# Another order of the steps in two attention stages of an eight-stage kernel on one Trainium2 core

## Chip, cores and metric

One core of one Trainium2 chip runs the whole program. The metric is the device time of the program in microseconds (us), the median of several executions; lower is better.

## What is computed

The reference is a stack of eight residual sublayers on x of shape (16, 128, 128), all in float32: four attentions, each followed by a feed-forward layer.

```python
x = x + tanh(g_xattn[0]) * attention0(layernorm(x), ctx, ctx)   # 16 heads of 8, window of 64
x = x + tanh(g_ffn[0])   * experts0(layernorm(x))               # 8 experts, top 2
x = x + tanh(g_xattn[1]) * attention1(ctx, layernorm(x))        # 8 heads of 64, rotary keys
x = x + tanh(g_ffn[1])   * experts1(layernorm(x))               # 16 experts, top 2, and a shared one
x = x + tanh(g_xattn[2]) * attention2(layernorm(x), ctx)        # 16 heads of 8, q, k, v projected
x = x + tanh(g_ffn[2])   * gated_layer(layernorm(x))
x = x + tanh(g_xattn[3]) * correlation(layernorm(x), ctx, ctx)
x = x + tanh(g_ffn[3])   * experts3(layernorm(x))               # 8 experts, top 2
```

The change concerns attention0 and attention2, "the first" and "the third" attention below. Both compute softmax(q kT / sqrt(8)) v for 16 heads of 8 over 128 queries and 128 keys for each of the 16 batches, and then a 128 x 128 output projection. The first masks scores further than 64 from the diagonal and takes q, k and v as they are. The third projects them first.

## The kernel before

Each stage is a block in which five engines run their own instruction lists, kept in step by semaphores alone. A stage treats one batch (128 tokens x 128 features) at a time and is written as a software pipeline by hand: `walk(engine, [(step, lag), ...])` issues for t = 0, 1, 2, ... each listed step in the listed order for batch t - lag. So the table of an engine sets which instruction stands behind which on that engine, and by how many batches the steps lie apart. One pass through a table is called a round; in the steady state every engine makes one round for each batch. An engine works in order: a step that waits holds everything behind it. The lags have a meaning only within one engine, since nothing but the semaphores ties the engines together.

Both attentions are `small_head_attention` (`project=False` for the first, `project=True` for the third). Its steps, with the lines of the profile:

- TensorE (PE): `in_T` transposes the normalised x (L585); `qkv` projects it in the third (L609, L610, L611, in this order q, k, v); `scores(0)` and `scores(2)` make the scores of heads 0 to 7 and 8 to 15 in PSUM banks 0, 1 and 2, 3 (L530, and the mask's product L527 ahead of it in the first); `probs(0)` and `probs(2)` transpose the exponentials (L556); `pv` multiplies with the values (L593); `output_transpose` (L543), `out_T` (L563) and `out` (L599) lead to the projected output; in the first, `next_T` (L571) transposes the normalised result, `logits` (L603) makes the router's logits of it and `ranks` (L284 to L287) counts tokens per expert.
- VectorE (DVE): `stats_in` (L240, L242; in the third with the addition of the last expert layer's two late results ahead of it, L352), `norm_in` (L252), `maximum(0)` and `maximum(1)` over the two halves of the scores (L629), `shift(0)` and `shift(1)`, which subtract the maximum and so free the PSUM banks (L638), `divide` (L646, L649), `add` of the residual (L654), `values` in the third (L685); in the first `stats_out`, `norm_out` (L252 into `routed_lines`), `chosen` (L261 to L267, the top two experts) and `placed` (L273, L277, their line numbers).
- ScalarE (ACT): the exponentials (L746), and copies out of PSUM, among them `queries` (in the third keys L774, then queries L780), `outputs` (L787), `out_T` (L758), `next_T` (L763), `logits` (L791) and `probs_out` (L753).
- GpSimd (POOL): `dev_in` and `dev_out` (the inverse deviations, L246, L248; in the third also a copy of the context, L701), `bias` (L705), `spread_keys` (L715: the keys times the head mask into a 128 x 512 tile), `spread_values` (L722), and DMAs by index: `sent` (L313, the routed lines of a batch, two of them) in the first and `fetched` (L345, the late results, two of them) in the third; `counted` (L300) in the first.

The scores have no second buffer. `scores(0)` of a batch waits for `shift(0)` of the batch before, and `scores(2)` for its `shift(1)`:

```python
wait(pe, s.keys, b + 1)
wait(pe, s.shifted, b * 2 + (first // 2 - 1))
```

`spread_keys` of batch b waits for both parts of the scores of batch b - 2, and in the third for the keys of batch b (`s.kT`). `fetched` of batch b waits until the late results of batch b - 2 are added. `chosen` waits for the logits that ACT has copied, `placed` and `counted` for the ranks, `sent` for the slots that `placed` writes.

Of the kernel before, what the change touches and what calls it, by code (L numbers as in the profile page):

```python
# [72 lines left out]
def split(ap, b):  # L73
    return ap.rearrange("p (a b) -> p a b", b=b)
# [375 lines left out]
def small_head_attention(nc, sems, k, tag, src, masked, project, w_out, tg, tgb, w_gate, n_gate, ld, a):  # L450
# [40 lines left out]
    with nc.Block() as block:  # L491
# [27 lines left out]
        def _(pe):  # L519
# [27 lines left out]
            def probs(first):  # L547
                def stage(b, sl):
                    wait(pe, s.exp, b + 1)
                    for g in range(first, first + 2):  # L550
                        wait(pe, s.pT, b * NG + (g - 1))
                        if g == 0:
                            wait(pe, s.ots, b)
                        for j in range(HG):
                            h = g * HG + j
                            last = nc.tensor.transpose(bank[:, PT + g % 2, j * T:(j + 1) * T],  # L556
                                                       k.e[:, sl, h * T:(h + 1) * T], c["ident"])
                        last.then_inc(s.ptr, 1)
                return stage
# [46 lines left out]
            def qkv(b, sl):  # L606
# [4 lines left out]
                nc.tensor.matmul(bank[:, MA, 384:512], ctxs[:, sl, :], k.w["wv2"], start=True, stop=True).then_inc(s.qkv, 1)  # L611

            pe.wait_ge(ld.weights[4 if project else 0], 16)
            walk(pe, [(out_T, 5), (scores(0), 2), (qkv, 1), (out, 5), (pv, 4), (scores(2), 2),
                  (probs(0), 3), (output_transpose, 4), (probs(2), 3), (in_T, 0)]
                 if project else
                 [(ranks, 7), (scores(0), 1), (logits, 6), (probs(0), 3), (output_transpose, 4), (in_T, 0), (probs(2), 3),
                  (out_T, 4), (scores(2), 1), (out, 4), (pv, 3), (next_T, 5)])

        @block.vector  # L620
        def _(dve):
            nc.vector.memset(vpad, 0.0).then_inc(s.padded, 1)
            dve.wait_ge(s.padded, 1)
            nc.vector.memset(vpad[:, :, :, DH:DH + 1], 1.0).then_inc(s.padded, 1)  # L624

            def maximum(half):
                def stage(b, sl):
                    wait(dve, s.scores, b * 2 + (half + 1))
                    nc.vector.tensor_reduce(mx[:, sl, 8 * half:8 * half + 8],  # L629
                                            bank[:, 2 * half:2 * half + 2, :].rearrange("p g (j t) -> p (g j) t", j=HG),  # L630
                                            AX.X, ALU.max).then_inc(s.max, 1)
                return stage

            def shift(half):
                def stage(b, sl):
                    wait(dve, s.max, b * 2 + (half + 1))
                    wait(dve, s.ptr, b * NG - NG)
                    nc.vector.tensor_tensor(split(k.e[:, sl, 1024 * half:1024 * half + 1024], T),  # L638
                                            bank[:, 2 * half:2 * half + 2, :].rearrange("p g (j t) -> p (g j) t", j=HG),
                                            over(mx[:, sl, 8 * half:8 * half + 8], T, 2), ALU.subtract).then_inc(s.shifted, 1)  # L640
                return stage

            def divide(b, sl):
# [12 lines left out]

            def stats_in(b, sl):
                if project:
                    add_late(dve, b)
                elif b % 4 == 0:  # L660
                    dve.wait_ge(ld.x[b // 4], 16)
                stats1(dve, at(k.x, b), sl, b + 1, s.xh)

            def norm_in(b, sl):
                wait(dve, s.xTp, b - 1)
                norm1(dve, xh[:, sl, :], at(k.x, b), sl, b + 1).then_inc(s.xh, 1)

            def stats_out(b, sl):
                wait(dve, s.added, b + 1)
                stats2(dve, at(k.x, b), sl, b + 1, s.xh2)  # L670

            def norm_out(b, sl):
                line_free(dve, s, ld, 0, b)
                norm2(dve, k.line[:, b % LINES, :, 0:D], over(k.x[:, b, :], 2, 1), sl, b + 1).then_inc(s.xh2, 1)

            def chosen(b, sl):
                choose(dve, b)

            def placed(b, sl):
                place(dve, b, bank[:, MA, 256:256 + n_gate])  # L680

            def values(b, sl):
                wait(dve, s.qkv, b + 1)
                wait(dve, s.q, b + 1)
                nc.vector.tensor_tensor(at(vtok, b), bank[:, MA, 384:512], k.rows["b_v"], ALU.add).then_inc(s.v, 1)  # L685

            walk(dve, [(shift(1), 4), (norm_in, 1), (stats_in, 0), (maximum(0), 3), (add, 6), (shift(0), 3),
                  (values, 2), (maximum(1), 3), (divide, 5)]
                 if project else
                 [(shift(0), 3), (add, 6), (stats_out, 6), (placed, 8), (maximum(1), 3), (stats_in, 0), (shift(1), 3),  # L690
                  (divide, 5), (norm_out, 6), (chosen, 7), (maximum(0), 2), (norm_in, 0)])

        @block.gpsimd
        def _(pool):
            pool.wait_ge(s.padded, 2)

            def dev_in(b, sl):
                dev1(pool, sl, b + 1)
                if project:
                    wait_apart(pool, k, s.qkv, b - 1)  # L700
                    nc.gpsimd.tensor_copy(ctxs[:, sl, :], at(k.ctxT, b)).then_inc(s.ctxs, 1)  # L701

            def bias(b, sl):
                wait_apart(pool, k, s.xh, b + 1)
                nc.gpsimd.tensor_tensor(at(k.x, b), at(k.x, b), tgb, ALU.add).then_inc(s.biased, 1)  # L705

            def dev_out(b, sl):
                dev2(pool, sl, b + 1)

            def spread_keys(b, sl):  # L710
                if project:
                    wait(pool, s.kT, b + 1)
                wait_apart(pool, k, s.scores, b * 2 - 2)
                keys = kT[:, sl, :] if project else at(k.ctxT, b)
                nc.gpsimd.tensor_tensor(kx[:, sl, :, :], over(keys, HG, 1), over(c["headmask"], T, 2),  # L715
                                        ALU.mult).then_inc(s.keys, 1)

            def spread_values(b, sl):
                if project:
                    wait(pool, s.v, b + 1)  # L720
                wait_apart(pool, k, s.pv, b - 1)
                nc.gpsimd.tensor_copy(vpad[:, sl, :, 0:DH], split(at(vtok, b), DH)).then_inc(s.vpad, 1)  # L722

            def counted(b, sl):
                count(pool, b)

            def sent(b, sl):
                if b == 0:
                    pool.wait_ge(ld.empty[0], 32 * (E0 + 1))
                send(pool, b)  # L730

            def fetched(b, sl):
                fetch(pool, b)

            if not project:
                begin(pool)
            walk(pool, [(fetched, -1), (dev_in, 0), (spread_values, 3), (spread_keys, 1), (bias, 4)]
                 if project else
                 [(dev_in, 0), (spread_keys, 0), (dev_out, 5), (bias, 0), (counted, 7), (spread_values, 3),
                  (sent, 8)])  # L740

        @block.scalar
        def _(act):
# [45 lines left out]
            def logits(b, sl):  # L789
# [1 line left out]
                nc.scalar.activation(at(k.logits, b)[:, 0:n_gate], bank[:, MB, 384:384 + n_gate],  # L791
                                     ACT.Copy).then_inc(s.logits_out, 1)

            walk(act, [(queries, 1), (outputs, 4), (probs_out, 3), (in_T, 0), (out_T, 4), (exps, 2)]
                 if project else
                 [(outputs, 4), (logits, 6), (probs_out, 3), (queries, 0), (out_T, 4), (exps, 2), (next_T, 5)])

# [1233 lines left out]
```

## Time and profile before

| | us |
|---|---|
| median of three executions (lowest, highest) | 1074.42 (1074.01, 1080.66) |
| the profiled execution | 1072.74 |
| its span in the profile | 1071.0 |
| PE busy | 818.7 (76%) |
| DVE busy | 648.2 (61%) |
| ACT busy | 500.8 (47%) |
| POOL busy | 437.2 (41%) |
| first attention, first DVE statistics to the last indexed send | 15.6 to 176.8 |
| third attention, first DVE memset to the last addition | 630.6 to 773.2 |

The time of the profiled execution is the whole program's; the span is from its first to its last instruction. Busy shares are averages over eight stages with different limits, so a stage is read by itself, through the rows of its own stretch. A stretch of the profile is named by its microseconds from the start of the span. PEld is TensorE's weight load, which runs ahead of the matmuls and whose starts follow one another more evenly, so distances on PE are read there.

### The profile page before, as it was taken

To read this page: it belongs to the slowest core of one execution; us is meant where nothing else is said; L and a number is where in the kernel's file an instruction comes from. 1 tells how busy PE (TensorE), PEld (TensorE's weight loads), DVE (VectorE), ACT (ScalarE), POOL (GpSimd) and SP (SyncE) were. 2 spreads that over 40 slices of the span, in tenths; PEclk is the share of its full clock that TensorE was granted. 3 is DMA by queue.
4 is the path that set the end of the run, shared out by engine and by line. 5 is a ranking of instruction groups with operands and counts; after the bars stand their busy time and mean duration, and the time that the engine had idled before them with its cause. 6 is when DMAs were issued, how large, how long until landed. Compare 5 with 4: busy or idle time off the path is not lost. (4 is left out here: it accounts for less than half of the span.)

```text
span 1071.0 us, 20849 instructions
## 1 busy us (share of the span) xinstructions
PE 818.7 (76%) x5970; PEld 588.4 (55%) x5984; DVE 648.2 (61%) x1891; ACT 500.8 (47%) x1403; POOL 437.2 (41%) x779
## 2 busy tenths in 40 slices
PE   4998882995789989898727949999787546259991
PEld 1556561663457777677515735666566335237771
DVE  5898973333357777777534438999598344334443
ACT  1565560552156656665504724777534122025552
POOL 3355644002334455653340036665265128803334
PEclk9999995998699999999958976999968765579996
DMA  8999601331000000000002530010001211122214
GB/s 276 369 403 340 230 22 34 83 79 38 11 11 11 7 17 22 16 17 12 16 26 58 117 78 21 17 22 12 1 2 40 79 41 36 44 57 59 58 36 130
DMA packets 68861, 78.93 MB, mean 74 GB/s; under 512 B 12432, under 2 KB 58144, under 8 KB 68496
## 3 DMA queue, kind: packets, MB, share of 16 engines
q1 hardware_dynamic: 59840, 62.74, 18.3%
q0 software_dynamic: 6368, 13.38, 4.4%
q10 hardware_dynamic: 2544, 1.48, 0.6%
q8 instruction: 53, 0.87, 0.4%
q14 instruction: 56, 0.46, 0.1%
HBM read 31.61 MB, written 45.96 MB: 72 GB/s over the span
## 5 line engine op out<-in xcount | busy, mean ns | idle before, releaser
L313 POOL DMA_INDIRECT routed_region<-routed_lines,line_slots x96 | 97.2, 1012 | 23.2 <-issue 22.6
L345 POOL DMA_INDIRECT late_results<-routed_region,line_slots x64 | 63.2, 987 | 97.8 <-DVE work_a L624 80.4
L248 POOL TENSOR_TENSOR small<-small,half_and_eps 128x1 f32<-128x1 f32 x160 | 92.3, 577 | 12.5
L753 ACT ACTIVATE probs_keymajor_a<-banks 128x512 f32<-128x512 f32 x128 | 70.0, 595 | 43.0 <-PE banks L556 43.0
L868 PE MATMUL banks<-work_a,weights_a 128*128 128x128 f32 x512 | 76.8, 295 | 15.5 <-ACT work_a L1084 9.7
L1244 PE MATMUL banks<-weights_f,block_feat_f 128*128 x156 | 83.7, 619 | 1.2 <-ACT block_feat_f L1296 0.9
L530 PE MATMUL banks<-work_a 32*128 32x512 f32 x256 | 81.1, 713 | 0.0
L629 DVE TENSOR_REDUCE small<-banks 128x8 f32<-128x1024 f32 x64 | 77.5, 1212 | 5.7 <-PE banks L530 5.6
L868 PEld LDWEIGHTS banks<-work_a,weights_a 128*128 128x128 f32 x512 | 65.3, 200 | 25.8 <-ACT work_a L1084 13.4
L638 DVE TENSOR_TENSOR exps_a<-banks,small 128x1024 f32<-128x1024 f32 x64 | 77.6, 1213 | 2.3 <-PE banks L556 1.9
L556 PE MATMUL banks<-consts,exps_a 128*128 128x128 f32 x512 | 72.5, 288 | 1.3 <-ACT work_a L787 1.3
L1261 PE MATMUL banks<-weights_f,block_hidden_feat_f 128*128 x468 | 65.8, 277 | 7.3 <-ACT block_hidden_feat_f L1316 7.1
L246 POOL TENSOR_TENSOR small<-small,half_and_eps 128x1 f32<-128x1 f32 x160 | 31.6, 198 | 94.8 <-DVE small L242 94.0
L556 PEld LDWEIGHTS banks<-consts,exps_a 128*128 128x128 f32 x512 | 59.4, 149 | 19.6 <-issue 15.9
L1426 DVE TENSOR_TENSOR block_hidden_f<-block_gate_f,banks 128x64 f32<-128x64 f32 (+1 forms) x86 | 26.8, 312 | 71.4 <-ACT block_gate_f L1302 70.4
L1479 POOL DMA_INDIRECT expert_results<-block_out_f,block_to_f x39 | 37.8, 970 | 76.5 <-DVE block_to_f L1436 42.9
L1316 ACT ACTIVATE block_hidden_feat_f<-banks,cols 128x128 f32<-128x128 f32 x156 | 44.7, 374 | 40.2 <-PE banks L1252 29.1
L1261 PEld LDWEIGHTS banks<-weights_f,block_hidden_feat_f 128*128 128x128 f32 x468 | 58.4, 192 | 9.0 <-issue 9.0
L746 ACT ACTIVATE exps_a<-exps_a 128x2048 f32<-128x2048 f32 x32 | 61.5, 1921 | 3.2 <-DVE exps_a L638 3.2
L1252 PEld LDWEIGHTS banks<-consts,block_hidden_f 128*128 128x128 f32 x281 | 37.5, 143 | 44.0 <-issue 28.2
L1077 ACT ACTIVATE probs_keymajor_a<-banks 128x512 f32<-128x512 f32 x64 | 34.9, 595 | 51.5 <-PE banks L894 51.5
L1096 ACT ACTIVATE exps_a<-banks,small 128x256 f32<-128x256 f32 x128 | 58.7, 492 | 0.0
(277 smaller groups left out, 2002.8 us busy)
## 6 DMA issues: line engine op xcount, KB each, us to landing
routed_region<-mid_a SPq DMA_DIRECT2D x52, 528.0 KB, 13.8
block_lines_f<-routed_region SPq DMA_DIRECT2D x125, 66.0 KB, 1.9
routed_region<-block_out_f SPq DMA_DIRECT2D x86, 64.0 KB, 1.8
weights_f<-in_weights_f SPq DMA_DIRECT2D x1, 4096.0 KB, 15.7
weights_f<-in_weights_f SPq DMA_DIRECT2D x3, 1024.0 KB, 12.4
shifted_rows<-work_a SPq DMA_DIRECT2D x16, 128.0 KB, 1.7
both_outs_f<-expert_results SPq DMA_DIRECT2D x4, 512.0 KB, 5.7
routed_region<-routed_lines,line_slots POOLq DMA_INDIRECT x96, 2.3
```

The lines of the kernel that those rows point to most:

```text
L248: nc.gpsimd.tensor_tensor(rstd[:, s, 1:2], rstd[:, s, 0:1], k.half[:, 0:1], ALU.pow).then_inc(sem.rstd, 1)
L313: nc.gpsimd.indirect_dma_start(k.regions[layer % 2], bass.IndirectOffsetOnAxis(k.slots[:, b, j:j + 1], 0), k.line[:, b % LINES, j, :], Non ...
L345: nc.gpsimd.indirect_dma_start(k.late[:, b % 2, j, :], None, k.regions[layer], bass.IndirectOffsetOnAxis(k.slots[:, b, j:j + 1], 0)).then_ ...
L530: last = nc.tensor.matmul(bank[:, g, :], qT[rows_, sl, :], kx[rows_, sl, :, :].rearrange("p j t -> p (j t)"), start=not masked, stop=True)
L556: last = nc.tensor.transpose(bank[:, PT + g % 2, j * T:(j + 1) * T], k.e[:, sl, h * T:(h + 1) * T], c["ident"])
L629: nc.vector.tensor_reduce(mx[:, sl, 8 * half:8 * half + 8], bank[:, 2 * half:2 * half + 2, :].rearrange("p g (j t) -> p (g j) t", j=HG), A ...
L638: nc.vector.tensor_tensor(split(k.e[:, sl, 1024 * half:1024 * half + 1024], T), bank[:, 2 * half:2 * half + 2, :].rearrange("p g (j t) -> ...
L746: nc.scalar.activation(k.e[:, sl, :], k.e[:, sl, :], ACT.Exp, scale=float(1 / np.sqrt(DH))).then_inc(s.exp, 1)
L753: nc.scalar.activation(k.pT[:, g * 512:(g + 1) * 512], bank[:, PT + g % 2, :], ACT.Copy).then_inc(s.pT, 1)
L868: last = nc.tensor.matmul(bank[:, MA, p * T:(p + 1) * T], k.w[weight][:, p * 128:(p + 1) * 128], kvT[:, sl, part * T:(part + 1) * T], star ...
L1244: nc.tensor.matmul(bank[:, 2 + m % 2, 0:wide], k.gotT[:, m % 2, :], ups[:, bass.ds(offs[m], wide)], start=True, stop=True).then_inc(s.up, 1)
L1261: last = nc.tensor.matmul(bank[:, 6 + m % 2, 0:D], k.hidT[:, m % 2, i * T:(i + 1) * T], downs[:, bass.ds(offs[m] + (down_at + i * D), D)], ...
```

## The change

Only the tables of `walk` are changed, for all four engines in both attentions; no step is edited, added or removed. In the third, the two parts of the scores now stand next to one another on PE, as do the two maxima and the two shifts on DVE; the fetch of the late results on POOL moves from one batch ahead of `dev_in` to two. In the first, `ranks` comes a round earlier on PE, `norm_in` on DVE a round later than `stats_in`, and `divide` behind `maximum(0)`.

```diff
-            walk(dve, [(shift(1), 4), (norm_in, 1), (stats_in, 0), (maximum(0), 3), (add, 6), (shift(0), 3),
-                  (values, 2), (maximum(1), 3), (divide, 5)]
+            walk(dve, [(shift(0), 3), (shift(1), 3), (divide, 5), (values, 2), (norm_in, 1), (maximum(0), 2),
+                       (maximum(1), 2), (add, 5), (stats_in, 0)]
...
-            walk(pool, [(fetched, -1), (dev_in, 0), (spread_values, 3), (spread_keys, 1), (bias, 4)]
+            walk(pool, [(dev_in, 2), (bias, 3), (spread_values, 4), (fetched, 0), (spread_keys, 2)]
...
```

Third attention, PE, one steady round; before:

```order
L563 MATMUL banks<-consts,work_a 128x128
L530 MATMUL banks<-work_a 128x512 x2
L609 MATMUL banks<-work_a,weights 128x128
L610 MATMUL banks<-work_a,weights 128x128
L611 MATMUL banks<-weights,work_a 128x128
L599 MATMUL banks<-weights,work_a 128x128
L593 MATMUL banks<-probs_keymajor_a,work_a 32x128 x16
L530 MATMUL banks<-work_a 128x512 x2
L556 MATMUL banks<-consts,exps_a 128x128 x8
L543 MATMUL banks<-consts,work_a 128x128 x4
L556 MATMUL banks<-consts,exps_a 128x128 x8
L585 MATMUL banks<-consts,work_a 128x128
```

The same round after the change:

```order
L530 MATMUL banks<-work_a 128x512 x4
L585 MATMUL banks<-consts,work_a 128x128
L563 MATMUL banks<-consts,work_a 128x128
L593 MATMUL banks<-probs_keymajor_a,work_a 32x128 x16
L609 MATMUL banks<-work_a,weights 128x128
L610 MATMUL banks<-work_a,weights 128x128
L611 MATMUL banks<-weights,work_a 128x128
L599 MATMUL banks<-weights,work_a 128x128
L556 MATMUL banks<-consts,exps_a 128x128 x8
L543 MATMUL banks<-consts,work_a 128x128 x4
L556 MATMUL banks<-consts,exps_a 128x128 x8
```

The projection of the next batch (L609 to L611) and the output projection (L599) stood between the two parts of the scores and now stand behind both, and behind `pv`.

Third attention, DVE, one steady round; before:

```order
L638 TENSOR_TENSOR exps_a<-banks,small 128x1024
L252 TENSOR_SCALAR work_a<-x_tok,small 128x128
L352 SCALAR_TENSOR_TENSOR x_tok<-late_results,expert_shares,x_tok 128x128 x2
L240 BN_STATS small<-x_tok 128x6
L242 BN_AGGR small<-small 128x2
L629 TENSOR_REDUCE small<-banks 128x8
L654 SCALAR_TENSOR_TENSOR x_tok<-banks,tanh_gates,x_tok 128x128
L638 TENSOR_TENSOR exps_a<-banks,small 128x1024
L685 TENSOR_TENSOR work_a<-banks,rows 128x128
L629 TENSOR_REDUCE small<-banks 128x8
L646 RECIPROCAL small<-banks 128x16
L649 TENSOR_TENSOR work_a<-banks,small 128x128
```

The same round after the change:

```order
L638 TENSOR_TENSOR exps_a<-banks,small 128x1024 x2
L646 RECIPROCAL small<-banks 128x16
L649 TENSOR_TENSOR work_a<-banks,small 128x128
L685 TENSOR_TENSOR work_a<-banks,rows 128x128
L252 TENSOR_SCALAR work_a<-x_tok,small 128x128
L629 TENSOR_REDUCE small<-banks 128x8 x2
L654 SCALAR_TENSOR_TENSOR x_tok<-banks,tanh_gates,x_tok 128x128
L352 SCALAR_TENSOR_TENSOR x_tok<-late_results,expert_shares,x_tok 128x128 x2
L240 BN_STATS small<-x_tok 128x6
L242 BN_AGGR small<-small 128x2
```

The addition of the residual (L654), which waits for `out`, stood between a maximum and a shift of the two different halves; now it stands right ahead of the late results (L352), and these ahead of the two shifts.

First attention, DVE, from `shift(1)` on; before:

```order
L638 TENSOR_TENSOR exps_a<-banks,small 128x1024
L646 RECIPROCAL small<-banks 128x16
L649 TENSOR_TENSOR work_a<-banks,small 128x128
L252 TENSOR_SCALAR routed_lines<-x_tok,small 128x2x128
L261 MAX top_values<-logits 128x8
L263 MAX_INDEX top_indices<-top_values,logits 128x8
L267 TENSOR_TENSOR one_hot<-top_indices,expert_numbers 128x2x8
L629 TENSOR_REDUCE small<-banks 128x8
L252 TENSOR_SCALAR work_a<-x_tok,small 128x128
L638 TENSOR_TENSOR exps_a<-banks,small 128x1024
L654 SCALAR_TENSOR_TENSOR x_tok<-banks,tanh_gates,x_tok 128x128
```

The same stretch after the change:

```order
L638 TENSOR_TENSOR exps_a<-banks,small 128x1024
L261 MAX top_values<-logits 128x8
L263 MAX_INDEX top_indices<-top_values,logits 128x8
L267 TENSOR_TENSOR one_hot<-top_indices,expert_numbers 128x2x8
L629 TENSOR_REDUCE small<-banks 128x8
L646 RECIPROCAL small<-banks 128x16
L649 TENSOR_TENSOR work_a<-banks,small 128x128
L252 TENSOR_SCALAR work_a<-x_tok,small 128x128
L638 TENSOR_TENSOR exps_a<-banks,small 128x1024
L273 TENSOR_TENSOR picked_slots<-one_hot,banks 128x2x8
L277 TENSOR_REDUCE line_slots<-picked_slots 128x2
L252 TENSOR_SCALAR routed_lines<-x_tok,small 128x2x128
```

The choice of experts (L261 to L267) stood behind the division; now the division (L646, L649) stands behind the choice and a maximum. On PE, in the same rounds, the logits (L603) follow `next_T` (L571) with one part of the scores and `in_T` between; after the change that stretch reads:

```order
L571 MATMUL banks<-consts,routed_lines 128x128
L527 MATMUL banks<-mask_bias 128x512 x2
L530 MATMUL banks<-work_a 128x512 x2
L585 MATMUL banks<-consts,work_a 128x128
L603 MATMUL banks<-weights_a,work_a 128x8
L556 MATMUL banks<-consts,exps_a 128x128 x8
L543 MATMUL banks<-consts,work_a 128x128 x4
L556 MATMUL banks<-consts,exps_a 128x128 x8
L284 MATMUL banks<-picks_so_far,ones_and_earlier 128x8
```

Before, L585 stood ahead of the second L556 and L284 right behind L571.

## Rows read from the trace of the kernel before

**Rows 1.** Busy time by stretch: steady rounds of the first and third attention.
```profile
46.60:139.50 92.90, 85.74 (x835) 55.22 (x844) 85.58 (x199) 58.26 (x109) 52.45 (x100) 0.98 0.85 311
664.00:757.80 93.80, 90.57 (x925) 61.38 (x917) 86.45 (x155) 71.40 (x128) 53.62 (x93) 1.00 0.07 16
```
**Rows 2.** Residual additions L654, first twelve of the first, first thirteen of the third.
```profile
L654 DVE SCALAR_TENSOR_TENSOR x_tok<-banks,tanh_gates,x_tok x12: 334/339/343, 46.6 to 139.5; 128x128 f32<-128x128 f32 x12
L654 DVE SCALAR_TENSOR_TENSOR x_tok<-banks,tanh_gates,x_tok x13: 341/342/343, 671.9 to 757.6; 128x128 f32<-128x128 f32 x13
```
**Rows 3.** Timeline of PEld in the third attention: start, duration, engine, line.
```profile
691.07 0.30 PEld L609 LDWEIGHTS banks<-work_a,weights 128*128 128x128 f32 x2 [0.76 <-issue]
...
691.73 0.30 PEld L599 LDWEIGHTS banks<-weights,work_a 128*128 128x128 f32 x2
692.15 0.81 PEld L593 LDWEIGHTS banks<-probs_keymajor_a,work_a 128*32 128x32 f32 x32
693.16 0.30 PEld L530 LDWEIGHTS banks<-work_a 32*128 32x128 f32 x4 [0.20 <-issue]
```
**Rows 4.** Timeline of PEld and ACT in the first attention.
```profile
74.82 0.14 PEld L563 LDWEIGHTS banks<-consts,work_a 128*128 128x128 f32 x1
...
75.56 0.30 PEld L530 LDWEIGHTS banks<-work_a 32*128 32x128 f32 x4 [0.42 <-issue]
76.61 0.30 PEld L599 LDWEIGHTS banks<-weights_a,work_a 128*128 128x128 f32 x2 [0.76 <-ACT work_a L758]
...
80.42 0.30 PEld L603 LDWEIGHTS banks<-weights_a,work_a 128*128 128x128 f32 x2 [0.76 <-issue]
...
80.84 0.18 ACT L791 ACTIVATE logits<-banks 128x8 f32<-128x8 f32 x1 [1.26 <-PE banks L603]
```
**Rows 5.** Timeline of DVE in the first attention, the same round.
```profile
74.14 0.26 DVE L646 RECIPROCAL small<-banks 128x16 f32<-128x16 f32 x1 [0.17 <-PE banks L543]
74.43 0.29 DVE L649 TENSOR_TENSOR work_a<-banks,small 128x128 f32<-128x128 f32 x1
...
74.96 0.16 DVE L261 MAX8 top_values<-logits 128x8 f32<-128x8 f32 x1
...
75.52 1.22 DVE L629 TENSOR_REDUCE small<-banks 128x8 f32<-128x1024 f32 x1
76.65 0.34 DVE L252 TENSOR_SCALAR work_a<-x_tok,small 128x128 f32<-128x128 f32 x1
```
**Rows 6.** Timeline: `out` on PE with nothing ahead of it, then the addition.
```profile
152.55 0.49 PE L599 MATMUL banks<-weights_a,work_a 128*128 128x128 f32 x2 [0.48 <-ACT work_a L758]
...
153.08 0.35 DVE L654 SCALAR_TENSOR_TENSOR x_tok<-banks,tanh_gates,x_tok 128x128 f32<-128x128 f32 x1 [0.51 <-PE banks L599]
```
**Rows 7.** Timeline of DVE in the third attention, late results and statistics.
```profile
691.36 0.74 DVE L352 SCALAR_TENSOR_TENSOR x_tok<-late_results,expert_shares,x_tok 128x128 f32<-128x128 f32 x2 [0.27 <-DMA late_results<-routed_region,line_slots]
692.18 0.29 DVE L240 BATCH_NORM_STATS2 small<-x_tok 128x6 f32<-128x128 f32 x1
...
692.61 1.19 DVE L629 TENSOR_REDUCE small<-banks 128x8 f32<-128x1024 f32 x1
```
**Rows 8.** Timeline of ACT and POOL in the third attention: keys, then their spreading.
```profile
692.68 0.35 ACT L774 ACTIVATE work_a<-banks,cols 128x128 f32<-128x128 f32 x1
...
693.11 1.04 POOL L715 TENSOR_TENSOR work_a<-work_a,consts 128x512 f32<-128x512 f32 x1 [2.10 <-ACT work_a L774]
```
**Rows 9.** Timeline, start of the third attention: POOL L715 and DVE L352 at once.
```profile
642.01 1.05 POOL L715 TENSOR_TENSOR work_a<-work_a,consts 128x512 f32<-128x512 f32 x1
642.52 1.07 DVE L352 SCALAR_TENSOR_TENSOR x_tok<-late_results,expert_shares,x_tok 128x128 f32<-128x128 f32 x2 [0.36 <-DMA late_results<-routed_region,line_slots]
```
**Rows 10.** Timeline, first attention: POOL L715 and DVE L252 at once.
```profile
84.84 1.04 POOL L715 TENSOR_TENSOR work_a<-ctx_feat,consts 128x512 f32<-128x512 f32 x1 [0.80 <-PE banks L530]
84.87 1.09 DVE L252 TENSOR_SCALAR work_a<-x_tok,small 128x128 f32<-128x128 f32 x1
```
**Rows 11.** The indexed sends L313 from 165 to 177 us.
```profile
L313 POOL DMA_INDIRECT routed_region<-routed_lines,line_slots x8: 962/962/1092, 166.6 to 175.9; - x8
```

More of the change, by code:

```diff
@@ L613, in _ @@
             pe.wait_ge(ld.weights[4 if project else 0], 16)
-            walk(pe, [(out_T, 5), (scores(0), 2), (qkv, 1), (out, 5), (pv, 4), (scores(2), 2),
-                  (probs(0), 3), (output_transpose, 4), (probs(2), 3), (in_T, 0)]
+            walk(pe, [(scores(0), 1), (scores(2), 1), (in_T, 0), (out_T, 4), (pv, 3), (qkv, 0), (out, 4),
+                      (probs(0), 2), (output_transpose, 3), (probs(2), 2)]
                  if project else
-                 [(ranks, 7), (scores(0), 1), (logits, 6), (probs(0), 3), (output_transpose, 4), (in_T, 0), (probs(2), 3),
-                  (out_T, 4), (scores(2), 1), (out, 4), (pv, 3), (next_T, 5)])
+                 [(scores(0), 1), (in_T, 0), (logits, 6), (probs(0), 3), (output_transpose, 4), (probs(2), 3),
+                  (ranks, 6), (out_T, 4), (scores(2), 1), (out, 4), (pv, 3), (next_T, 5)])
         @block.vector
@@ L685, in values @@
                 nc.vector.tensor_tensor(at(vtok, b), bank[:, MA, 384:512], k.rows["b_v"], ALU.add).then_inc(s.v, 1)
-            walk(dve, [(shift(1), 4), (norm_in, 1), (stats_in, 0), (maximum(0), 3), (add, 6), (shift(0), 3),
-                  (values, 2), (maximum(1), 3), (divide, 5)]
+            walk(dve, [(shift(0), 3), (shift(1), 3), (divide, 5), (values, 2), (norm_in, 1), (maximum(0), 2),
+                       (maximum(1), 2), (add, 5), (stats_in, 0)]
                  if project else
-                 [(shift(0), 3), (add, 6), (stats_out, 6), (placed, 8), (maximum(1), 3), (stats_in, 0), (shift(1), 3),
-                  (divide, 5), (norm_out, 6), (chosen, 7), (maximum(0), 2), (norm_in, 0)])
+                 [(norm_out, 8), (stats_in, 0), (add, 7), (maximum(1), 4), (stats_out, 7), (shift(1), 4),
+                  (chosen, 8), (maximum(0), 3), (divide, 6), (norm_in, 1), (shift(0), 3), (placed, 8)])
         @block.gpsimd
@@ L736, in _ @@
                 begin(pool)
-            walk(pool, [(fetched, -1), (dev_in, 0), (spread_values, 3), (spread_keys, 1), (bias, 4)]
+            walk(pool, [(dev_in, 2), (bias, 3), (spread_values, 4), (fetched, 0), (spread_keys, 2)]
                  if project else
-                 [(dev_in, 0), (spread_keys, 0), (dev_out, 5), (bias, 0), (counted, 7), (spread_values, 3),
-                  (sent, 8)])
+                 [(dev_out, 7), (counted, 8), (spread_values, 5), (bias, 4), (spread_keys, 1), (sent, 8),
+                  (dev_in, 0)])
         @block.scalar
@@ L792, in logits @@
                                      ACT.Copy).then_inc(s.logits_out, 1)
-            walk(act, [(queries, 1), (outputs, 4), (probs_out, 3), (in_T, 0), (out_T, 4), (exps, 2)]
+            walk(act, [(in_T, 0), (out_T, 4), (outputs, 3), (queries, 0), (probs_out, 2), (exps, 1)]
                  if project else
-                 [(outputs, 4), (logits, 6), (probs_out, 3), (queries, 0), (out_T, 4), (exps, 2), (next_T, 5)])
+                 [(out_T, 5), (exps, 3), (next_T, 6), (outputs, 4), (queries, 0), (logits, 6), (probs_out, 3)])
 def latent_attention(nc, sems, k, ld):
```

## The prediction, made before the changed kernel ran

> **What bounds the kernel now.** I read the stretches first, then one steady round of each stage in the timeline, engine by engine. In the steady rounds of both stages PE and DVE are each busy over 92% of the time [rows 1]: 85.74 and 85.58 of 92.90 us in the first attention, 90.57 and 86.45 of 93.80 us in the third. A busy PE says little, so what counts is the loop of waits that repeats each round. The residual additions mark the rounds [rows 2]. In the first, twelve of them stand in 92.9 us, 8.45 us a round. In the third, thirteen stand in 85.7 us, 7.14 us a round.
>
> In the first, DVE hardly waits. Its largest loss is a collision: `norm_in` takes 0.34 us [rows 5], but 1.09 us when it starts just behind POOL's `spread_keys` [rows 10], and the DVE instruction behind it starts when POOL's ends. One such pair stands there, and there are four between the first and the twelfth addition, so 4 x 0.75 = 3.0 us. The granted clock of 0.98 in that stretch [rows 1] means about 3.7 us at the lower level, worth at most 1.9 us; I take 1.5 and keep it in both kernels. That leaves (92.9 - 3.0 - 1.5) / 11 = 8.04 us for a plain round.
>
> No instruction is added, so all costs below come from what stands behind what. They are worked out against the profiled execution, 1072.7 us with a span of 1071.0, which lies 1.7 us under the median; the difference is then put on the median, 1074.4.
>
> **Third attention, rounds.** The new order closes one long loop. DVE's `shift(1)` must end before PE's `scores(2)`; behind these PE has `in_T`, `out_T`, `pv`, `qkv` and only then `out`; DVE's `add` waits for `out`, and behind `add` stand the late results, the statistics and both shifts. Step by step: the first shift 1.13 and the second 1.22 and a hand-over of 0.04 [rows 5, 6] (a pass over 1024 columns lasts 1.22, its successor starts 1.13 after it); one part of the scores 1.05 [rows 4]; two transposes 0.14 each [rows 4]; `pv` 1.01, `qkv` 0.66 [rows 3]; `out` to `add` 0.53 [rows 6]; `add` 0.3 (0.34 less some overlap); late results 0.82 and statistics 0.43 [rows 7]. The sum is 7.5 us, against 7.14 now. Before, `out` was issued right behind `qkv` and ahead of `pv`, and DVE had two passes of other work on either side of `add`, so DVE's own work and not this loop set the round. The wait for the late results' DMA, 0.27 us in the row of rows 7, goes, since they are fetched a round earlier; that gain is swallowed by the loop.
>
> **Third attention, a collision in each round.** Count from the load of `qkv`. Its third product is loaded at 0.44 and ends at 0.44 + 0.49 + 0.04 = 0.97 (products as in rows 6); ACT's keys follow, and POOL's `spread_keys` starts 0.43 after them [rows 8], at 1.40, since POOL waits for the keys already now, 2.10 us in that row. It runs to 2.44. On DVE `add` starts at 0.66 + 0.53 = 1.19 and the first late addition at about 1.46. So each round `spread_keys` and the late additions want to run together. Where they did so at the start of the stage [rows 9], the pair of additions took 1.07 us instead of 0.74 [rows 7], with POOL 0.51 us ahead; with POOL only 0.06 ahead I expect the first addition to wait for nearly all of the 1.04 us, as `norm_in` did in rows 10. Should the addition start first, the second of the pair meets the same wait. The bounds are 0 and 1.0 us a round; I take 0.8, nearest to rows 10. The round is then 8.3 us.
>
> The Trainium skill, SBUF — State Buffer, section "Who interferes with whom", states that a DVE instruction with two SBUF inputs contends with a GpSimd instruction that reads SBUF, and that whichever issues first blocks the other for its whole length. L352 has two such inputs. Rows 9 agree in kind (0.33 us more). By the rule the wait is what is left of POOL's 1.04 us, about 1.0; without it the round would stay at 7.5.
>
> **Third attention, sum.** Eleven rounds of 8.3 and a last one without late results, statistics, projection and collision, 8.3 - 0.82 - 0.43 - 0.66 - 0.8 = 5.6, make 96.9 us between first and thirteenth addition, against 85.7: +11.2. Ahead of the first addition the pipeline fills at the lower clock, with both parts of the scores in a row ahead of all else: I take +1, bounds -1 and +4. At the end, the second shift of the last batch stands right behind the first instead of behind a maximum (1.13), the values and a division, some 1.9 us in all by the like rows of rows 5: -2. Sum +10.
>
> **First attention, rounds.** DVE's own list gets shorter waits, but here too a new loop closes, since `divide` now stands behind `chosen`, and `chosen` needs the logits of the same round: `out` 0.42 and `pv` 1.01 [rows 3], `next_T` with the mask to the scores' load 0.74, scores 1.05, `in_T` 0.14, logits to ACT 0.42, ACT 0.18 and 0.04 [rows 4], `chosen` 0.56, `maximum(0)` 1.13, reciprocal 0.29, quotient 0.29 and 0.04 [rows 5], `out_T` to the next scores 0.74, scores 1.05 [rows 4]. The sum is 8.10 us, 0.06 more than a plain round now: +0.7 over eleven. In this loop PE waits at `out_T` and DVE at `chosen`. The collision with `norm_in` goes: `spread_keys` is released by the scores' end, 0.29 + 0.33 + 0.74 + 1.2 = 2.6 us behind the reciprocal (1.2 is an estimate: the 1.05 of the scores and a hand-over), while `norm_in` starts 0.5 us behind it and `norm_out` 2.2 us behind it, both ahead of POOL: -3.0.
>
> **First attention, end.** POOL ends with eight sends, 166.6 to 175.9, 1.33 apart [rows 11], four batches that it could not send earlier because `sent` stood a round behind `counted`. Now both have one lag, and two batches are left: -5.3 at best. But `norm_out` of the last batch stands behind `placed` of the one before, and the last batch's own transpose, logits, choice, ranks and slots come in sequence ahead of its two sends. I take -2, bounds 0 and -5.3. Sum of the first: -4.3.
>
> Together +5.7 us: 1078.4 on the profiled execution, 1080.1 on the median.
>
> **Rivals.** (A) The late additions aren't held. For it: one row alone shows them held, and by 0.33 us, and a shift of 0.4 us of `spread_keys` would miss them. Against it: rows 10, where the wait is nearly whole. Then eleven times 0.8 goes: 1071.3. (B) In the first, `norm_out` meets `spread_keys`: it is only 0.4 us ahead, and `counted`, `spread_values` or `bias` on POOL may hold `norm_in` long enough. It decides once DVE loses 0.4 us between division and `norm_out`. Then DVE's list of 7.5 and a wait of 0.9 make 8.4: +3.3, 1083.4. (C) The other side, clearly slower: PE waits about 1.4 us in each round of the third (8.3 less 0.966 x 7.14 = 6.9 of work, rows 1 and 2), and its granted clock, 1.00 now [rows 1], falls to the lower of its two levels, 1.2 GHz. PE's part of the loop is 3.5 us, so a round at that clock costs up to 3.5 more; 2 us for six of the rounds is +12, 1092. Against it: the waits are short and PE is busy four fifths of the time. It decides if the clock falls for more than two rounds. (D) Both loops are shorter than I read them (a step released earlier): the first near 7.7 and the third near 7.0 without a collision, 1061. The waits in the code speak against it.
>
> **Numbers.** Forecast 0.46, A 0.27, B 0.12, C 0.09, D 0.06. The forecast's own bounds: the collision 0.5 to 1.0 (-3, +2), the fill (-2, +3), the first's end (-3, +2): 1075 to 1085. The range takes in A and most of B: 1068 to 1088. This kernel's measurement can tell about 1% from no change, 10.7 us. Faster by more: D and little else, 0.06. Slower by more, above 1085: C and part of B and of the forecast's upper end, 0.17. Within 1%: 0.77.
>
> **What would show it.** In the third: additions about 8.3 us apart; `add` preceded by a wait for L599; L352 pairs of some 1.5 us; L715 starting within 0.2 us of them; no wait for the late DMA; PE idle ahead of L530. In the first: L261 waiting for L791 each round, rounds of 8.1 us, no L252 over 0.6 us, and fewer sends behind the last addition. L352 pairs of 0.74 us would make A right; rounds under 7.4 in the third or under 7.9 in the first would show a loop wrong; a granted clock under 0.95 in the third would be C.

## The result and the profile after

The changed kernel takes 1087.96 us (median of 8, 1083.34 to 1095.48), the kernel before 1074.61 us in the same series (8 runs, 1072.96 to 1080.66). The ratio is 1.0124, 95% interval 1.0097 to 1.0150: the change makes the kernel slower by 13.4 us. The profiled execution took 1095.48 us, the slowest of the eight and 7.5 above their median, with a span of 1093.7.

The stretches that answer to [rows 1], of after; columns as there, the granted clock third from the end:

```profile
46.60:134.00 87.40, 84.74 (x817) 53.22 (x830) 80.33 (x199) 58.96 (x109) 55.39 (x104) 1.00 0.92 331
664.00:781.00 117.00, 101.69 (x885) 69.13 (x883) 95.12 (x160) 71.26 (x125) 53.31 (x95) 0.87 0.06 13
```

The first attention's clock is full and its twelve additions stand in 87.2 us instead of 92.9, 7.92 a round (8.00 in most). In the third the clock fell from 1.00 to 0.87, and thirteen additions stand in 110.9 us instead of 85.7.

One round of the third on DVE, the answer to [rows 7], then the POOL instruction beside it:

```profile
708.36 0.35 DVE L654 SCALAR_TENSOR_TENSOR x_tok<-banks,tanh_gates,x_tok 128x128 f32<-128x128 f32 x1 [0.52 <-PE banks L599]
708.62 1.53 DVE L352 SCALAR_TENSOR_TENSOR x_tok<-late_results,expert_shares,x_tok 128x128 f32<-128x128 f32 x2
710.19 0.29 DVE L240 BATCH_NORM_STATS2 small<-x_tok 128x6 f32<-128x128 f32 x1
...
710.62 2.33 DVE L638 TENSOR_TENSOR exps_a<-banks,small 128x1024 f32<-128x1024 f32 x2
```

```profile
708.59 1.03 POOL L715 TENSOR_TENSOR work_a<-work_a,consts 128x512 f32<-128x512 f32 x1 [2.32 <-ACT work_a L774]
```

The pair L352 takes 1.53 us instead of 0.74, with L715 0.03 us ahead of it. `add` waits for L599, and no wait for the late DMA is left. That is the predicted round. The same round and the next one on PE:

```profile
706.15 1.08 PE L593 MATMUL banks<-probs_keymajor_a,work_a 128*32 128x128 f32 x32
...
711.97 2.98 PE L530 MATMUL banks<-work_a 32*128 32x512 f32 x8 [1.37 <-DVE exps_a L638]
...
715.50 1.94 PE L593 MATMUL banks<-probs_keymajor_a,work_a 128*32 128x128 f32 x32
717.37 0.80 PE L609 MATMUL banks<-work_a,weights 128*128 128x128 f32 x2
```

PE waits 1.37 us for the shifts; in the scores behind that wait everything begins to take nearly twice as long (`pv` 1.94 instead of 1.08). The clock comes back later and falls again, but not behind every such wait. Of nine waits of 1.35 us or more in the stretch 664 to 781, seven are followed by a fall within 3 us. Two are not: the one of 1.49 us that ends at 703.6 and the one of 1.35 us that ends at 741.2, as the first and the last of these rows show (the middle one is the round that starts at 711.97):

```profile
703.60:711.90 8.30, 6.99 (x70) 4.71 (x70) 7.64 (x14) 5.64 (x10) 4.27 (x8) 1.00 0.08 17
712.00:723.00 11.00, 10.25 (x72) 6.83 (x73) 7.60 (x14) 5.80 (x10) 4.78 (x9) 0.69 0.06 14
741.20:749.50 8.30, 7.00 (x70) 4.73 (x70) 7.59 (x14) 5.64 (x10) 4.61 (x9) 1.00 0.08 17
```

So the additions follow one another in 8.2 to 8.5 us (four rounds, full clock) or in 9.9 to 11.2 (seven rounds). The waits of the stretch 664 to 781 (in total, times, longest):

```profile
DVE x_tok L654 <- PE banks L599: 19.9, 12, 3.3
...
PE banks L530 <- DVE exps_a L638: 15.1, 12, 1.5
```

In sum, against the profiled execution of before: the first attention's last addition came 3.9 us and its last send 6.6 us earlier; at the third's first transpose (L585) 0.8 us of that were left, the rest was given back in the layers between; the third's first addition came 1.9 us earlier, then +25.2 us to the thirteenth, -1.4 to the last, +0.7 behind: +22.7, as the spans say. The medians show 13.4 of it.

### The profile page after: what moved, and what is told of

It reads as the page before. It is cut to its first block and busy times, and to the rows that moved or that the text cites. A ratio compares the mean times of both kernels' runs of the same rounds, so it can differ in the third digit from the quotient of the medians.

```text
span 1093.7 us, 20849 instructions
## 1 busy us (share of the span) xinstructions
PE 836.7 (77%) x5970; PEld 602.3 (55%) x5984; DVE 650.8 (60%) x1891; ACT 503.7 (46%) x1403; POOL 436.4 (40%) x779
## 5 line engine op out<-in xcount | busy, mean ns | idle before, releaser
L313 POOL DMA_INDIRECT routed_region<-routed_lines,line_slots x96 | 96.8, 1008 | 25.8 <-issue 21.7
L345 POOL DMA_INDIRECT late_results<-routed_region,line_slots x64 | 63.2, 987 | 100.7 <-DVE work_a L624 83.2
L530 PE MATMUL banks<-work_a 32*128 32x512 f32 x256 | 78.0, 723 | 19.1 <-DVE exps_a L638 17.4
L556 PE MATMUL banks<-consts,exps_a 128*128 128x128 f32 x512 | 72.9, 289 | 0.9 <-ACT work_a L787 0.8
L556 PEld LDWEIGHTS banks<-consts,exps_a 128*128 128x128 f32 x512 | 61.5, 151 | 5.7 <-issue 1.9
L1041 POOL TENSOR_TENSOR work_a<-work_a 128x512 f32<-128x512 f32 x16 | 20.2, 1265 | 96.7 <-issue 80.3
```

The costliest lines, as they stand in the source:

```text
L313: nc.gpsimd.indirect_dma_start(k.regions[layer % 2], bass.IndirectOffsetOnAxis(k.slots[:, b, j:j + 1], 0), k.line[:, b % LINES, j, :], Non ...
L345: nc.gpsimd.indirect_dma_start(k.late[:, b % 2, j, :], None, k.regions[layer], bass.IndirectOffsetOnAxis(k.slots[:, b, j:j + 1], 0)).then_ ...
L530: last = nc.tensor.matmul(bank[:, g, :], qT[rows_, sl, :], kx[rows_, sl, :, :].rearrange("p j t -> p (j t)"), start=not masked, stop=True)
```

## The experiments

Each ratio is to the kernel before on the same chip, with its 95% interval. Four series ran on four chips: E1 to E4, E5 to E8, E9 to E11, E12. The trace also has the time at which each semaphore is raised; "released" below is that time.

**E1, E2: one attention each.** The tables of before were put back in the third (E1) or in the first (E2).

> The first attention's tables are the new ones, the third's are those of before. Theory 1 (the gain of the first attention is real and stays): its last addition and last send come 4 and 6.6 us earlier, as in the trace of after, and the whole is 6 us faster than before, 1068 to 1069. Theory 2 (what is won there is given back in the expert layer and the second attention, as 3.1 of 6.6 us were in after's trace by the start of the second expert layer, and 5.9 by its end): 1073 to 1075.

> The third attention's tables are the new ones, the first's are those of before. Theory 1 (the two parts add up): after minus before is +13.4 us in the medians, and with the first's -6.6 out it is +19 to +20, 1094. Theory 2 (my forecast's sizes, +10 for the third): 1084 to 1085. In the trace: rounds of 8.2 us with a full TensorE clock and of 9.9 with half of it in part, for theory 1; 8.3 throughout for theory 2.

E1: 1.0004 (0.9981 to 1.0026). E2: 1.0172 (1.0150 to 1.0194). So the loss is the third's: 18.6 us, near the 19 to 20 of theory 1. The first's gain was missing, and not for the reason expected: its last addition came at 167.2 us, not at 160.6, with 2.9 us lost among the first twelve additions and 3.1 in the last four. Two things stand out in it. In two rounds `norm_out` (L252) took 1.27 and 1.25 us beside `spread_keys`, rounds of 9.5 and 9.6: rival B, in part. And in the last rounds ACT's `next_T` started long after PE's transpose:

```profile
146.46 0.33 PE L571 MATMUL banks<-consts,routed_lines 128*128 128x128 f32 x1
148.54 0.39 PE L603 MATMUL banks<-weights_a,work_a 128*128 128x8 f32 x2 [1.75 <-ACT work_a L763]
```

```profile
148.21 0.28 ACT L763 ACTIVATE work_a<-banks 128x128 f32<-128x128 f32 x1 [2.19 <-PE banks L571]
```

In after's trace the transpose ended at 143.06 and the same ACT step began at 143.10. Here 1.4 us pass with no instruction between. `pv`, ahead of the transpose, was released 1.5 us after its start in eight rounds and 2.5 to 2.9 in the last four, where after has 1.12 throughout. POOL at that time, in E1:

```profile
145.27 1.05 POOL L313 DMA_INDIRECT routed_region<-routed_lines,line_slots  x1 [0.88 <-DVE line_slots L277]
146.62 0.96 POOL L313 DMA_INDIRECT routed_region<-routed_lines,line_slots  x1 [0.30 <-issue]
```

The second send ends at 147.58, and `pv` and the transpose are released at 148.15 and 148.18.

**E3, E4: the collision and the clock apart.** Both on the changed kernel.

```diff
 E3, spread_keys in the third:
+                    wait(pool, s1.stats, min(b + 2, B) if isinstance(b, int) else b + 2)
 E4, scores(0) in the third, ahead of its wait for shift(0):
+                    if project and first == 0 and b >= 2:
+                        wait(pe, s.pT, (b - 2) * NG + 3)
+                        for _ in range(5):
+                            nc.tensor.matmul(bank[:, PT, 0:T], c["ident"], c["ident"], start=True, stop=True)
```

> As after, but in the third attention spread_keys also waits for the statistics of the next batch, so it cannot run beside the late additions. Nothing is left out. Theory 1 (the collision costs 0.8 us in each round, on the loop): L352 pairs of 0.74 us, rounds of 7.5 us where the granted clock is full, and 11 x 0.8 = 9 us less than after in the whole, 1079. Theory 2 (the wait only moves: the shifts behind the statistics, which read PSUM and a small SBUF tile, are held by spread_keys instead, or the keys come late for the scores): first L638 over 1.5 us or rounds of 8.3 us, and the time of after. Either way it shows whether the clock of 0.86 recovers when the rounds get shorter.

> As after, but in the third attention PE makes five products of the identity with itself into bank 4 (about 1.1 us at full clock) in the wait ahead of the scores, after the third copy of the probabilities; their result is overwritten and enters nothing. Theory C (PE's wait of 1.4 us in each round lets the granted clock fall, and that makes rounds of 9.9 out of 8.3): granted clock 0.98 to 1.00 in the third, rounds of 8.3 to 8.5 us, 7 to 13 us less than after. Rival (the clock's fall has nothing to do with this wait, and the fillers only take time): clock 0.86 as now, rounds of 10 us and more, not faster than after.

E3: 0.9995 (0.9981 to 1.0008). E4: 1.0092 (1.0067 to 1.0117). A stretch of steady rounds, 674 to 758, of after, E3 and E4:

```profile
674.00:758.00 84.00, 73.51 (x617) 50.07 (x614) 65.81 (x113) 48.93 (x87) 40.57 (x68) 0.84 0.07 16
```

```profile
674.00:758.00 84.00, 76.70 (x772) 52.47 (x773) 75.62 (x143) 61.56 (x112) 47.42 (x84) 1.00 0.07 17
```

```profile
674.00:758.00 84.00, 80.50 (x802) 58.97 (x800) 76.80 (x131) 56.22 (x101) 44.92 (x79) 1.00 0.07 16
```

With the filler the clock is full and ten of eleven rounds are 8.38 us (one 8.73): the forecast's round (8.3) is there, collision and all. E4 in the timeline of DVE (L658 is `add` in its numbering):

```profile
698.53 0.35 DVE L658 SCALAR_TENSOR_TENSOR x_tok<-banks,tanh_gates,x_tok 128x128 f32<-128x128 f32 x1 [0.57 <-PE banks L603]
698.80 1.53 DVE L352 SCALAR_TENSOR_TENSOR x_tok<-late_results,expert_shares,x_tok 128x128 f32<-128x128 f32 x2
```

Without the collision (E3) the pair is short, the clock is full without any filler, and the rounds are 7.6. PE's wait of 1.37 us ahead of the scores is gone; its longest wait in a round is now one of 0.7 us ahead of `probs(0)`, for ACT's `outputs` (L788 in its numbering):

```profile
696.83 0.35 DVE L654 SCALAR_TENSOR_TENSOR x_tok<-banks,tanh_gates,x_tok 128x128 f32<-128x128 f32 x1 [0.62 <-PE banks L599]
697.09 0.73 DVE L352 SCALAR_TENSOR_TENSOR x_tok<-late_results,expert_shares,x_tok 128x128 f32<-128x128 f32 x2
```

```profile
697.45 1.07 PE L556 MATMUL banks<-consts,exps_a 128*128 128x128 f32 x8 [0.71 <-ACT work_a L788]
```

So on one chip: E2 to E4 is the clock, 1.0172 to 1.0092, 8.6 us, known to some 3 or 4 us by the intervals; E4 to E3 is 1.0092 to 0.9995, 10.5 us. Of these the eleven rounds, 0.76 us shorter each, are 8.4 us: the collision. Another 1.4 us lie in the last four intervals, where the collision costs nothing (after has 5.62 us there as E3 has, E4 7.31): they are the filler's own price, and by as much E2 to E4 understates the clock. (E3 and E4 have the first attention's new tables, worth nothing on this chip by E1; the changed kernel itself was not run on it.) My expectation for E3 had the collision right, 9 us, and left the clock open; that came on top: E2 to E3 is 19.1 us for one wait on POOL.

**E5: the sends away from `pv`** (first attention new, third of before).

```diff
-                 [(dev_out, 7), (counted, 8), (spread_values, 5), (bias, 4), (spread_keys, 1), (sent, 8),
-                  (dev_in, 0)])
+                 [(dev_out, 7), (sent, 9), (counted, 8), (spread_values, 5), (bias, 4), (spread_keys, 1),
+                  (dev_in, 0)])
```

> The first attention's new tables and the third's of before, but POOL's sends stand right behind dev_out, with lag 9, so that they are issued between two runs of pv and not beside one. In e1's trace pv's release (its semaphore, by which ACT's copy of its result starts) came 1.5 us after pv's start in the rounds and 2.5 to 2.9 in the last four, each time 0.54 to 0.6 us behind a start or end of a send, while pv's own matmuls were issued as ever. Theory 1 (an indirect send in flight on POOL holds pv's release): 1.12 us in every round, the last four additions 6 us apart or less in the mean instead of 7.4, and 3 to 5 us less than e1, 1075. Theory 2 (it is the chip, or spread_keys beside pv): 1.5 us and over stays, and the time of e1 or up to 2 us more, since the last sends come a round later.

E5: 0.9910 (0.9882 to 0.9938), last addition at 159.8, `pv` released after 1.12 us each time. This alone proves little, since on this chip E8 shows no late release either, with the sends where the change has them. The proof is in E9 to E11 below, which share a chip.

**E6, E7: two ways to shorten the third's loop** (first attention of before).

```diff
 E6, DVE and POOL:
-            walk(dve, [(shift(0), 3), (shift(1), 3), (divide, 5), (values, 2), (norm_in, 1), (maximum(0), 2),
-                       (maximum(1), 2), (add, 5), (stats_in, 0)]
+            walk(dve, [(shift(0), 3), (shift(1), 3), (stats_in, 0), (divide, 5), (values, 2), (norm_in, 1),
+                       (maximum(0), 2), (maximum(1), 2), (add, 5)]
-            walk(pool, [..., (fetched, 0), (spread_keys, 2)]
+            walk(pool, [..., (fetched, -1), (spread_keys, 2)]
 E7, PE:
-            ... (in_T, 0), (out_T, 4), (pv, 3), (qkv, 0), (out, 4), ...
+            ... (in_T, 0), (out_T, 4), (qkv, 0), (out, 4), (pv, 3), ...
```

> The first attention's tables are those of before, the third's the new ones with two edits: on DVE the late additions and the statistics stand right behind the second shift instead of behind add, and POOL fetches the late results a round earlier. That takes 0.74 and 0.47 us out of the loop from add to the scores, and the late additions away from spread_keys. Theory 1 (the loop of 7.5 us and the collision set the rounds): rounds of 7.0 to 7.1 us, L352 pairs of 0.74, granted clock 1.00, and 3 to 5 us less than before. Rival (some other wait behind it, for norm_in or the keys, sets 7.5 us or more): rounds of 7.5 and over, 3 us or more above before.

> The first attention's tables are those of before, the third's the new ones, but PE issues qkv and out ahead of pv instead of behind it. Keys and add keep their distance, so the collision stays. Theory 1 (pv's 1.01 us lies on the loop from the scores to add): rounds 1.0 us shorter at full clock, 7.3, PE's wait ahead of the scores 0.4 us instead of 1.4, and so the clock stays at 1.00: 18 to 20 us less than with the new third alone, 1080 where before is 1080.7. Rival (the scores wait for something else, the keys or the shifts behind other work): rounds stay at 8.2 and more.

E6: 0.9956 (0.9939 to 0.9973), rounds of 7.37, pairs of 0.74, clock 1.00. Its thirteen additions stand in 85.9 us, as before's (85.7; before's 7.14 is the mean of nine rounds of 7.35 and three shorter ones), so the rounds are not where it gains. Its last four additions span 13.9 us, not 15.2, and from the first L585 to the first addition it takes 29.0 us, before 33.2 (on another chip). The rounds missed the 7.0: PE waits 0.9 us a round for `norm_in`.

E7: 1.0148 (1.0113 to 1.0184), rounds of 8.15. The expectation failed, in its time and in that the collision would stay: the collision is gone (pairs of 0.73), but two new waits stand in its place, here of 674 to 758:

```profile
PE banks L609 <- ACT work_a L768: 13.8, 11, 1.3
PE banks L556 <- ACT work_a L787: 8.1, 10, 0.8
```

`qkv` now stands right behind the two transposes and waits for ACT's copy L768, which stands behind the exponentials (1.9 us); `pv` had covered that wait. I had costed moving `pv` at its own length and overlooked what it hid. And its clock, in the same stretch:

```profile
674.00:758.00 84.00, 62.24 (x720) 45.67 (x723) 72.38 (x133) 55.43 (x103) 45.67 (x80) 1.00 0.08 18
```

PE is busy 62 of 84 us, less than in after, and keeps the full clock. So it is not the amount of waiting that brought the clock down. In E7 no wait of this stretch is over 1.26 us and there are two a round; in after and E2 most rounds have one of 1.35 us or more in one piece. That the length of one piece decides isn't shown: in after two such waits had no fall behind them, and in E2 one of 1.11 us had.

**E8: the changed kernel again**, with no edit.

> The changed kernel itself, beside the others on one chip. Theory 1 (the parts add up: the first alone 1.0004, the third alone 1.0172): 1.0176 on a chip where the first attention's gain is lost to pv's late release; on one where it isn't, 1.012. Rival (they interact, the third's clock depending on where the stage begins): outside 1.010 to 1.020.

E8: 1.0098 (1.0067 to 1.0130), clock 0.87 in 664 to 758, rounds of 8.2 to 11.2. On this chip the first attention's gain is whole (last addition at 160.5, last send at 169.2). It lies just outside the 1.010 to 1.020 that theory 1 allowed, with an interval that holds the 1.012 of the result. With 0.991 for the first (E5, its sends moved) and 1.0172 for the third (E2, another chip), the product is 1.008, inside the interval: the parts add up as far as this can tell. The first's gain also reaches the third here: its first L585 starts at 634.4 us in E8 and at 642.9 and 644.3 in E6 and E7, which have the old first attention (one execution each).

**E9 to E11: both edits, and E1 once more beside them.** E9 is the changed kernel with the edits of E5 and E6. E11 is E1 unedited. E10 is E9 with

```diff
-            walk(dve, [(shift(0), 3), (shift(1), 3), (stats_in, 0), (divide, 5), (values, 2), (norm_in, 1),
+            walk(dve, [(shift(0), 3), (shift(1), 3), (norm_in, 1), (stats_in, 0), (divide, 5), (values, 2),
```

> Changed kernel with both edits: the sends behind dev_out in the first attention, the late additions and statistics behind the second shift (late results fetched a round earlier) in the third. Theory 1 (the two gains are independent): the product of the two ratios, 0.991 x 0.9956 = 0.987, some 14 us less than before. Rival (a shorter first attention is given back in the expert layers and the second attention, whose clock falls elsewhere): 0.991 to 0.996.

> As e9, and in the third attention norm_in stands right behind the two shifts, ahead of the late additions. In the trace of the version with the early statistics, PE waits 0.9 us in each round of 7.37 for norm_in (L585 for L252). Theory 1 (this wait is on the loop): rounds of 6.9 to 7.0 us, bounded by PE's and DVE's own work, and 4 to 5 us less than e9. Rival (the wait moves to another step, as it did when out was issued ahead of pv): rounds of 7.2 and more, the time of e9 within 2 us.

> The first attention's new tables alone once more (e1), beside the others. In e1's job pv's release came late and the ratio was 1.0004; in the next job the whole change showed no late release, and the same tables with the sends apart gave 0.991. Theory 1 (the late release is what cost e1 its gain, and moving the sends brings little by itself): without a late release here 0.991 to 0.993, with one 1.000. Theory 2 (the sends' place is worth the 9 us whether or not the release is late): 0.998 to 1.001 in either case.

E9: 0.9899 (0.9868 to 0.9930), between the 0.987 of its theory 1 and the 0.991 of its rival, with both inside the interval. E10: 0.9930 (0.9906 to 0.9954). E11: 1.0013 (0.9984 to 1.0042). In E11 `pv` is released 1.5 us after its start in the rounds and 2.3 to 2.8 in the last four, as in E1; in the first attention of E9 and E10, on the same chip, 1.12 each time. So moving the sends removes the late release there. Whether their place matters without it is answered by E8, whose last addition is early with the sends unmoved. On the chips of after and of E8 it never showed, though the sends stood beside `pv` there too; why one chip has it and another not stays open. That it alone cost E11 its gain isn't shown: E9's third differs too.

E10 went as its rival said in its rounds (7.45 us, E9 7.37); its time is 3 us above E9's, not within 2, with intervals that overlap. The wait ahead of L585 stayed at 1.0 us and only changed its name, to `values` (L685), which frees the bank that `in_T` writes:

```profile
PE banks L585 <- DVE work_a L685: 8.2, 8, 1.1
```

**E12: `values` early as well.**

```diff
-            walk(dve, [(shift(0), 3), (shift(1), 3), (norm_in, 1), (stats_in, 0), (divide, 5), (values, 2),
+            walk(dve, [(shift(0), 3), (shift(1), 3), (values, 2), (norm_in, 1), (stats_in, 0), (divide, 5),
```

> As e10, and values stands right behind the two shifts too, ahead of norm_in. In e10's trace PE still waits 1.0 us a round ahead of L585, now for values (L685), which frees the bank that in_T writes; DVE waits 0.43 us a round, ahead of add. Theory 1 (that wait is the last on the loop, and DVE's own list of 7.45 - 0.43 = 7.0 us bounds the round next): rounds of 7.0 to 7.1 us, PE's wait ahead of L585 under 0.2 us, 4 us less than e10 on one chip, a ratio of 0.985 to 0.990. Rival (the wait moves once more): rounds of 7.3 and more, ratio 0.990 to 0.993.

E12: 0.9876 (0.9846 to 0.9905), 1061.96 us beside 1075.12 of before on its chip: faster than both kernels and the lowest ratio of all, though its interval overlaps E9's. The ratio is theory 1's, the rounds of 7.25 lie half-way to the rival's. PE's wait ahead of `in_T` is gone and a shorter one has come, for `divide`:

```profile
PE banks L563 <- DVE work_a L649: 5.1, 8, 0.6
```

## Why the prediction held in the loop and the collision, and missed the clock

- **Third, the loop and the collision: right.** The sum gave a round of 8.3 us; with the clock held (E4) it is 8.38, and 0.76 of it is the collision (0.8 taken). Without it, 7.6 (E3; 7.5 summed). Rival A (not held) is out. The Trainium skill, SBUF — State Buffer, section "Who interferes with whom", agrees in that L352 waits for L715, and not in how long: L352 ends 0.15 us after L715 does, so it is held about 0.79 us, less than the whole 1.03, and the measurement decides.
- **Third, the clock: wrong, and this is the step that failed.** The sum left PE's clock at 1.00 in the third. Rival C, in which it falls, had 0.09, with "the waits are short and PE is busy four fifths of the time" against it. The clock fell in seven of eleven rounds; eleven rounds of 9.57 instead of 8.38 are +13 us in the trace, and 8.6 us in the comparison E2 to E4. Its price had been put at +12 (2 us in six rounds); its chance was misjudged. The share of busy time was the wrong thing to look at (E7: 62 of 84 us busy and full clock).
- **Fill and end of the third:** predicted +1 and -2. The first addition came 1.9 us earlier than before, from 0.8 us earlier at the first L585 (32.1 us between them instead of 33.2), so the fill was -1.1. The last four additions, 13.9 us instead of 15.2, give -1.4.
- **First, rounds: the loop right, the gain too small.** 8.10 predicted, 8.00 measured in most rounds (7.92 in the mean), and no `norm_in` collision. In after's waits L261 waits for L791 in nine of ten rounds, as the loop says. The gain was put at 2.3 us and is 5.7 in the trace: the mean round is 0.18 us under 8.10, 2.0 us in eleven, and the 1.5 us that the sum kept in both kernels for the lower clock went too (0.98 before, 1.00 after). Rival B didn't come on the chips of after and E8; in three later series `norm_out` met `spread_keys` in one to four rounds (1.15 to 1.27 us instead of 0.41).
- **First, end: smaller than forecast.** I took -2 of at most -5.3. From the twelfth addition to the last send it was 36.4 us and is 35.3, with three sends fewer behind the last addition: -1.0. Rounds and end together gave -6.6 us, not -4.3, in after's trace. In E1 and E11 the gain was gone, with `pv`'s late release in both.
- **Sum:** +5.7 forecast, +13.4 measured. By the series the third is worth +18.6 us (E2) against the forecast's +10; without the clock's part it is +9.5 (E4 against E1, known to some 3 us), close to the forecast's +10. The first was worth -9.7 us in E5 and nothing in E1, against -4.3. That the sum adds the first's gain in full was not safe either: in after's trace 0.8 of 6.6 us were left at the third's start. The measured 1087.96 lies 8.0 us above the forecast and inside the range by 0.04 us. That is luck: the range had been drawn for A and most of B, and C, the rival that came in part, was priced outside it, at 1092. "Within 1%" had 0.77; what came, slower by more, had 0.17.

## What to carry to other kernels

When a change opens a wait on TensorE in each round, price the matmuls behind it at both clock levels, even if the engine is busy over four fifths of the time. Here one wait of about 1.4 us a round went with a falling clock, and two of 1.26 and 0.8 us a round, with a larger sum, did not. A step that is moved takes its cover with it: look up what waited behind it unseen (E7, E10). And look for a collision that can be removed by ordering the two steps: one wait on POOL (E3) took away the collision and the fall of the clock, 19 us on its chip. The new order of the third alone, without the collision, is then worth nothing (E3 0.9995, E1 1.0004).

## What was not expected of the hardware

In two series (E1, E3, E4 and E11; not in E2, E9 and E10, whose sends stand elsewhere) `pv`'s result in the first attention was released 0.5 to 0.6 us after the start or end of an indirect send on POOL in nearly every round, up to 2.9 us after `pv` began, with its matmuls issued as ever. In after the sends start as near to `pv`, 0.17 us ahead of its release, and the release stays at 1.12 us. E3 shows it in the third too: with L345 beside it `pv` was released after 2.1 us, in the last batches without a fetch after 1.12; in E9 and E10 it was 1.3 to 1.5 us beside L345 there. The mechanism is open.

`norm_out`'s L252 took 1.25 to 1.27 us instead of 0.41 where it started 0.06 to 0.09 us ahead of L715 (E1, E3), and L715 kept its 1.04: here the DVE instruction is held even when it is the first by so little, where the prediction took it that the first to start holds the other.
